# A graph network on one core: waits ahead of GpSimd's gathers are replaced by a small memset ahead of every gather

## The chip, the cores and the metric

One core of a Trainium2 chip runs the whole program. It has five engines with queues of their own: TensorE (matmuls and transposes into PSUM banks), VectorE, ScalarE, GpSimd (which here issues the gathers, as indirect DMAs whose descriptors it writes itself) and SyncE (plain DMAs). Engines wait for one another through semaphores, counters that an instruction increments when it is done. The metric is the device time of one launch in microseconds (us), the median over several runs.

## The reference, cut to what matters

3125 nodes with 128 features; 53125 edges, sorted by their destination node. Two attention layers over the edges, each behind a LayerNorm and a ReLU and with a residual connection:

```
h = relu(layernorm(x));  x = x + layer0(h, src, dst)
    layer0: h = x W^T (8 heads x 16)
            e = leaky_relu(a_src[src] + a_dst[dst]);  alpha = softmax of e over the edges of a node
            out = sum over the edges of a node of alpha * h[src]
h = relu(layernorm(x));  x = x + layer1(h, src, dst, edge_attr)
    layer1: score = q[dst] . k[src] / 4 + edge_attr We;  attn = softmax over the edges of a node
            out = layernorm((sum of attn * v[src]) Wo + residual)
```

For every edge the features of its source node are needed: 544 bytes a row in layer 0 (features and a score part), 1024 bytes in layer 1 (keys and values). That is the gather.

## The kernel before, in words

The edges lie in tiles of 128, one edge a partition. A tile is visited once for each block of 125 destination nodes that it touches; there are 440 visits a layer. 16 visits make a group, 4 visits a quarter: `GROUPS` is 28, the last group has 2 quarters. Each visit has one gather of 128 rows out of a table in HBM into its place in `G` (L532), so there are 440 gathers a layer, 880 in all, 16 in a full group.

`G` holds three groups (`UNROLL = 3`). Group g takes the place of group g - 3, and may fill a quarter of it when VectorE has read that quarter for the last time, in `weigh` (L1418), which increments `pv_ready`. VectorE runs `weigh` of group r = g - 2 in its step g.

All compute engines go through the same steps, one a group, with three groups in work at a time (`run_groups`): in step g the new group g gets its scores, the group g - 1 its maxima and exponentials, the group g - 2 its weighted sums. The order of the work in a step is written out by hand for each engine. What the rows below name:

- TensorE: `spread_ids` (L829, layer 0) or `one_hot_T` (L836, layer 1), counted by `t_done`; `expand` (L851 in layer 0, L849 in layer 1), counted by `expanded`, which brings the values of the destination nodes to the edges; the transposed scores (L883, L884, `scoreT`); the small products `hop1` (L900) and `hop2` (L912); `sums` (L865), 6 batches a group over the 16 visits, counted by `mm_done`.
- VectorE: `add` (L1441), one for each visit, waits for `mm_done` of its batch and adds it to the nodes' sums `acc`; `weigh` (L1418); CCM (L1348) waits for `hop2`; in layer 1 `qk_product` (L1238) waits for a quarter's gathers and for `expand`, `qk_sum` (L1247) sums it, and `sc` (L1291) is the group's score; in layer 0 `score_sum` (L1279) waits for all gathers of the group, and `sc` (L1288) comes behind it.
- ScalarE: copies out of PSUM (ST, L646), one-hot tiles S (L636, L640), exponentials (L673).

GpSimd issues the gathers of a layer in order (`gathers`). Ahead of a quarter it waits for `pv_ready`. Ahead of the first gather of each quarter `pace` has it wait as well for counts of TensorE: `expanded`, `scoreT`, `hop1`, `hop2`, `t_done` of the group before, and `mm_done` of the group that held the place in `G`. These waits aren't needed for the data; the waits on `pv_ready`, on the tables and on the indices are, and stay. Ahead of the gathers of layer 0 GpSimd fills a small tile `pad_i` (1 partition, 2 x 130 columns of int32; L425 to L427), which ScalarE's queue sends to HBM at the start; nobody reads it afterwards.

Of the kernel before, what the change touches and what calls it, by code (L numbers as in the profile page):

```python
# [38 lines left out]
UNROLL = 3  # L39
# [23 lines left out]
NB = len(BATCHES)  # L63
# [12 lines left out]
def gnn_kernel(nc, x, src, dst, edge_attr, w0, att, bias0, wq, bq, wk, bk, wv, bv, we, be, wo, bo, gamma,  # L76
# [3 lines left out]
    def sb(name, shape, dt=F32):  # L80
        return ctx.enter_context(nc.sbuf_tensor(name, shape, dt))

    def sem(name):
        return ctx.enter_context(nc.semaphore(name))

    def wait(eng, s, value):

        if not isinstance(value, int) or value > 0:
            if isinstance(s, Signal):
                eng.wait_ge(s.s, s.base + value)  # L90
            else:
                eng.wait_ge(s, value)

    with ctx:
# [111 lines left out]
        pad_i = sb("pad_i", [1, 2, P + 2], I32)  # L206
# [49 lines left out]
        s_ebout, s_ebin, s_ebt, s_ebe = sem("bias_rows_out"), sem("bias_rows_in"), sem("bias_transposed"), sem("bias_copied")  # L256
        s_ebfin = sem("bias_complete")
        s_out = sem("out_written")
        s_bias3 = sem("bias_parts")
        s_kvb, s_qmm, s_q, s_gain, s_res = (sem(n) for n in (  # L260
            "keys_values_complete", "queries_projected", "queries_complete", "gain_applied", "result"))
# [21 lines left out]
        L = [Layer(0), Layer(1)]  # L283
# [8 lines left out]
        def quarters(g):  # L292

            return 0 if g < 0 or g >= GROUPS else LASTQ if g == GROUPS - 1 else 4
# [119 lines left out]
        def _(pool):  # L414
            n = [0]
# [53 lines left out]
                pool.dma_start(WeBD[ED * c:ED * c + ED, c, :], we).then_inc(s_r, 16)  # L469
            pool.memset(acc[:, :, :], 0.0).then_inc(s_acc0, 1)  # L470

            def pace(n, g, v):

                s, r, q = L[n], g - UNROLL, g - 1
                if v % 4:
                    return
                if g == 0:
                    if v == 12 and n == 0:
                        wait(pool, s["t_done"], 4)
                    return  # L480
                if n == 0:
                    if v == 0:
                        wait(pool, s["expanded"], 4 * q + 2)
                        if r >= 0:
                            wait(pool, s["mm_done"], NB * r + 3)
                    if v == 4:
                        wait(pool, s["expanded"], 4 * q + 4)
                        if r >= 0:
                            wait(pool, s["mm_done"], NB * r + 5)
                    if v == 8:  # L490
                        wait(pool, s["scoreT"], g)
                        if r >= 0:
                            wait(pool, s["mm_done"], NB * r + 6)
                    if v == 12:
                        wait(pool, s["hop1"], g)
                        if r >= 0:
                            wait(pool, s["mm_done"], NB * r + 7)
                elif r < 0:
                    if v == 0:
                        wait(pool, s["expanded"], 4 * q + 1)  # L500
                    if v == 4:
                        wait(pool, s["hop1"], q)
                    if v == 8:
                        wait(pool, s["expanded"], 4 * q + 3)
                else:
                    if v == 4:
                        wait(pool, s["hop1"], q)
                        if r >= 0:
                            wait(pool, s["mm_done"], NB * r + 1)
                    if v == 8:  # L510
                        wait(pool, s["hop2"], q)
                        wait(pool, s["t_done"], 4 * q + 3)
                        if r >= 0:
                            wait(pool, s["mm_done"], NB * r + 3)
                    if v == 12:
                        wait(pool, s["expanded"], 4 * q + 3)
                        wait(pool, s["t_done"], 4 * q + 4)
                        if r >= 0:
                            wait(pool, s["mm_done"], NB * r + 4)

            def gathers(n, table, w):
                s = L[n]

                for g in range(GROUPS):
                    u = g % UNROLL
                    for j in range(quarters(g)):
                        if n == 1 and g == UNROLL - 1 and j == 0:
                            pool.wait_ge(s_ebt, VK * H)
                        wait(pool, s["pv_ready"], 4 * (g - UNROLL) + j + 1)
                        for v in range(QV * j, QV * j + QV):  # L530
                            pace(n, g, v)
                            pool.indirect_dma_start(  # L532
                                G[:, u, v, 0:w], None, table,
                                bass.IndirectOffsetOnAxis(ap=idx_all[:, g * GV + v:g * GV + v + 1], axis=0)
                            ).then_inc(s_gath[u][j], 16)

            pool.wait_ge(s_idx0, 1)
            pool.wait_ge(s_tab[0], 32 * len(CHUNKS))
            gathers(0, table0, W0)
            pool.wait_ge(s_ebout, 16)  # L540
            pool.wait_ge(s_bz, 16)
# [5 lines left out]
            pool.memset(acc[:, :, :], 0.0).then_inc(s_acc0, 1)  # L547
            pool.wait_ge(s_tab[1], 32 * PAIRS)
            gathers(1, table1, W1)


# [1077 lines left out]
```

## Time and profile before

| | |
|---|---|
| median of 3 runs | 1584.45 us (1582.59 to 1594.63) |
| span of the profiled execution | 1585.9 us |
| GpSimd (POOL) busy | 883.4 us, 56% of the span |
| TensorE (PE) busy | 1020.5 us, 64% |
| VectorE (DVE) busy | 934.6 us, 59% |
| ScalarE (ACT) busy | 640.0 us, 40% |
| bytes moved by DMA | 110.35 MB, 70 GB/s |

Of the profiled execution only the span is known; it stands 1.45 us above the median of the runs. "Idle" is the time an engine stood still directly before an instruction, and the name behind the arrow is the releaser, what the profile holds for the end of that wait; "issue" means that nothing it shows ended it, "remote" that the count came from another core or an unknown queue. Matmuls are pipelined, and the ends of their records are modelled.

### The profile page before, as it was taken

The page shows a single profiled execution, that of the slowest core. Times are in us where ns is not written, and L with a number is a line of the kernel's source. Part 1 is how long each engine was busy: PE and PEld are TensorE (multiplying, and loading weights), DVE is VectorE, ACT ScalarE, POOL GpSimd, SP SyncE. Part 2 cuts the span into 40 slices and gives each one's busy share as a digit, 9 for nine tenths or more (in the row PEclk, how much of TensorE's full clock was granted, in tenths as well). Part 3 has the DMA queues.
Part 4 walks back from the last instruction along what each step waited for, and adds up shares of the span by engine and source line. Part 5 has one row for each costly group of instructions (what it writes and reads, how often), then busy time and mean ns, then how long its engine had stood idle before and what let it go on. Part 6 is the DMA issues. An engine that isn't in the chain of part 4 may idle for free.

```text
span 1585.9 us, 21105 instructions
## 1 busy us (share of the span) xinstructions
PE 1020.5 (64%) x4985; PEld 863.7 (54%) x4985; DVE 934.6 (59%) x3002; ACT 640.0 (40%) x1699; POOL 883.4 (56%) x926
## 2 busy tenths in 40 slices
PE   5456666666665766666554577666766676676765
PEld 4345555555554555445354466565655566566664
DVE  6445656556565565557813455656565656656578
ACT  5524334243342433422554234444443434344414
POOL 5766666666666566551046566656666565666500
PEclk9655555555656565566766666877777777777676
DMA  6321222222222222222133222222222222232201
GB/s 138 72 66 43 66 46 66 48 63 45 67 47 67 45 65 47 58 84 57 49 94 95 73 84 84 84 80 80 84 84 84 80 82 81 84 88 83 80 1 41
DMA packets 54202, 110.35 MB, mean 70 GB/s; under 512 B 16876, under 2 KB 30848, under 8 KB 53956
## 3 DMA queue, kind: packets, MB, share of 16 engines
q0 software_dynamic: 36288, 91.12, 22.6%
q1 hardware_dynamic: 16483, 17.39, 4.0%
q8 instruction: 46, 0.75, 0.2%
q14 instruction: 72, 0.59, 0.1%
q10 hardware_dynamic: 1313, 0.50, 0.1%
HBM read 100.60 MB, written 8.81 MB: 69 GB/s over the span
## 4 chain that ended last, share of the span: by engine, by line
DVE 16%; PE 16%; another core or an unknown queue 10%; issue 9%; ACT 2%; DVEq 2%
PE bank L865 6%; PE bank L849 6%; DVE acc L1441 4%; DVE PV L1418 3%; DVE prod L1238 2%; PE bank L836 1%; PE bank L912 1%; DVE raw L1247 1%; DVE halves L1087 1%; PE bank L900 1%; DVEq L1441 1%; ACT S L636 1%; DVEq L1220 0%; DVEq L90 0%
## 5 line engine op out<-in xcount | busy, mean ns | idle before, releaser
L532 POOL DMA_INDIRECT G<-table,idx_all x880 | 857.1, 974 | 544.5 <-issue 280.3
L865 PE MATMUL bank<-PV,S 128*125 128x144 f32 x1760 | 449.5, 416 | 209.5 <-DVE acc L1441 104.4
L865 PEld LDWEIGHTS bank<-PV,S 128*125 128x125 f32 x1760 | 373.9, 287 | 236.1 <-issue 134.9
L1441 DVE TENSOR_TENSOR acc<-acc,bank 125x144 f32 x880 | 260.4, 296 | 339.3 <-remote 191.7
L636 ACT ACTIVATE S<-iota_n,lid 128x125 f32<-128x125 f32 x880 | 275.7, 386 | 0.7 <-issue 0.7
L849 PE MATMUL bank<-qe,ST 125*128 x880 | 182.0, 378 | 87.3 <-DVE prod L1238 80.7
L849 PEld LDWEIGHTS bank<-qe,ST 125*128 125x128 f32 x880 | 164.1, 279 | 96.7 <-issue 95.8
L1418 DVE TENSOR_TENSOR PV<-G,PV 128x512 f32<-128x512 f32 x220 | 151.2, 688 | 23.4 <-issue 22.8
L646 ACT ACTIVATE ST<-bank 125x512 f32<-125x512 f32 x110 | 63.6, 598 | 248.4 <-remote 197.6
L640 ACT ACTIVATE S<-S,ones 128x500 f32<-128x500 f32 x220 | 156.6, 712 | 7.3
L836 PE MATMUL bank<-ident,S 128*125 128x128 f32 x440 | 89.8, 340 | 52.5 <-ACT S L640 31.9
L836 PEld LDWEIGHTS bank<-ident,S 128*125 128x125 f32 x440 | 79.1, 248 | 58.8 <-ACT S L640 35.1
L1228 DVE TENSOR_SCALAR ST<-bank,vcol 125x512 bf16<-125x512 f32 x110 | 81.5, 743 | 32.1 <-remote 27.6
L673 ACT ACTIVATE EP<-DD 128x256 f32<-128x256 f32 (+1 forms) x56 | 20.3, 363 | 191.2 <-DVE DD L1382 191.2
L1238 DVE TENSOR_TENSOR prod<-bank,G 128x512 f32<-128x512 f32 x110 | 74.5, 678 | 30.4 <-PE bank L849 27.1
L1348 DVE TENSOR_TENSOR CCM<-bank,Vsel 128x32 f32<-128x32 f32 x56 | 10.7, 191 | 118.6 <-remote 104.4
L688 ACT ACTIVATE AL<-bank 125x8 f32<-125x8 f32 x56 | 9.9, 177 | 165.9 <-PE bank L957 99.5
L1247 DVE TENSOR_REDUCE raw<-prod 128x32 f32<-128x512 f32 x110 | 74.3, 675 | 1.1
L912 PE MATMUL bank<-D,HselT 8*128 8x16 f32 x224 | 54.4, 358 | 28.8 <-DVE D L1334 27.9
L912 PEld LDWEIGHTS bank<-D,HselT 8*128 8x128 f32 x224 | 48.6, 299 | 42.4 <-DVE D L1334 29.1
L829 PE MATMUL bank<-lid_ring,ones_b 1*125 1x512 bf16 x110 | 53.2, 576 | 9.3 <-ACT attrT L684 5.4
L924 PE MATMUL bank<-WeBD,attrT 128*128 128x32 f32 x208 | 49.1, 400 | 5.6 <-DVE CCM L1348 5.6
(219 smaller groups left out, 1093.8 us busy)
## 6 DMA issues: line engine op xcount, KB each, us to landing
G<-table,idx_all POOLq DMA_INDIRECT x880
prod<-in_edge_attr_dram SPq DMA_DIRECT2D x8, 672.0 KB
table<-G SPq DMA_DIRECT2D x12, 224.0 KB
bias_rows<-qe SPq DMA_DIRECT2D x1, 1664.0 KB
table<-h0b SPq DMA_DIRECT2D x8, 178.5 KB
out_dram<-G SPq DMA_DIRECT2D x8, 168.0 KB
prod<-in_edge_attr_dram SPq DMA_DIRECT2D x8, 90.0 KB
xs<-in_x_dram SPq DMA_DIRECT2D x1, 504.0 KB
```

Of the source, the lines that this page charges most:

```text
L532: pool.indirect_dma_start(G[:, u, v, 0:w], None, table, bass.IndirectOffsetOnAxis(ap=idx_all[:, g * GV + v:g * GV + v + 1], axis=0)).then_ ...
L636: last = act.activation(S[:, u, v, :], iota_n[:, 0:BN], ACT.Abs, bias=lid[:, bass.ds(g * GV + v, 1)], scale=-1.0)
L640: act.activation(S[:, u, QV * j:QV * j + QV, :], S[:, u, QV * j:QV * j + QV, :], ACT.Relu, bias=ones[:, 0:1], scale=-1.0).then_inc(s.sem[" ...
L836: last = pe.transpose(tp[j % 2][0:BN, k * P:k * P + P], S[:, u, QV * j + k, :], ident[:, :])
L849: last = pe.matmul(ex[j % 2][:, k * F:k * F + F], ST[:, v, :], nodes[:, bass.ds(off, F)], start=True, stop=True)
L865: last = pe.matmul(sums_bank(p)[0:BN, at:at + H * SLOT], S[:, ur, v, :], PV[:, v, :, :].rearrange("p h k -> p (h k)"), start=True, stop=True)
L912: last = pe.matmul(sm[:, 64 + GV * k:64 + GV * k + GV], HselT[:, :, :].rearrange("p v h -> p (v h)"), d[:, k, k:k + GV], start=True, stop= ...
L1228: ve.tensor_scalar(ST_b[:, QV * j:QV * j + QV, :], tp[j % 2][0:BN, :].rearrange("p (v e) -> p v e", v=QV), node, None, op0=ALU.is_equal).t ...
L1238: ve.tensor_tensor(prod[:, j % 2, :].rearrange("p (v f) -> p v f", v=QV), ex[j % 2][:, :].rearrange("p (v f) -> p v f", v=QV), G[:, u, QV ...
L1247: ve.tensor_reduce(raw[:, QV * j:QV * j + QV, :].rearrange("p v h -> p (v h)"), prod[:, j % 2, :].rearrange("p (c d) -> p c d", d=DH), AX. ...
L1418: ve.tensor_tensor(PV[:, QV * j:QV * j + QV, :, 0:DH], rows, PV[:, QV * j:QV * j + QV, :, DH:DH + 1].to_broadcast([P, QV, H, DH]), ALU.mul ...
L1441: ve.tensor_tensor(a, a, o, ALU.add).then_inc(s.sem["acc_added"], 1)
```

## The change

`pace` and its calls are taken out. In its place, ahead of every gather, stands `space(260)`: a wait for the memset before it, and a memset of 260 columns of one partition of `pad_i`, which increments a new semaphore. The other waits ahead of gathers stay as they are, and so does every other engine.

```diff
@@ semaphores
+        s_space = sem("spacer_set")
@@ gpsimd
-            def pace(n, g, v):
-
-                s, r, q = L[n], g - UNROLL, g - 1
-                if v % 4:
-                    return
-                if g == 0:
-                    if v == 12 and n == 0:
-                        wait(pool, s["t_done"], 4)
-                    return
-                if n == 0:
-                    if v == 0:
-                        wait(pool, s["expanded"], 4 * q + 2)
-                        if r >= 0:
-                            wait(pool, s["mm_done"], NB * r + 3)
-                    if v == 4:
-                        wait(pool, s["expanded"], 4 * q + 4)
-                        if r >= 0:
-                            wait(pool, s["mm_done"], NB * r + 5)
...
-                else:
-                    if v == 4:
-                        wait(pool, s["hop1"], q)
-                        if r >= 0:
-                            wait(pool, s["mm_done"], NB * r + 1)
-                    if v == 8:
-                        wait(pool, s["hop2"], q)
-                        wait(pool, s["t_done"], 4 * q + 3)
-                        if r >= 0:
-                            wait(pool, s["mm_done"], NB * r + 3)
...
+            spaces = [0]
+
+            def space(width):
+
+                wait(pool, s_space, spaces[0])
+                pool.memset(pad_i[0:1, :, :].rearrange("p a b -> p (a b)")[:, 0:width], 0).then_inc(s_space, 1)
+                spaces[0] += 1
@@ gathers
                         for v in range(QV * j, QV * j + QV):
-                            pace(n, g, v)
+                            space(260)
                             pool.indirect_dma_start(
```

## Rows read from the trace of the kernel before

**Rows 1.** Costliest groups: line engine op, xcount | busy, mean ns | idle before, releaser.
```profile
L532 POOL DMA_INDIRECT G<-table,idx_all x880 | 857.1, 974 | 544.5 <-issue 280.3
...
L1238 DVE TENSOR_TENSOR prod<-bank,G 128x512 f32<-128x512 f32 x110 | 74.5, 678 | 30.4 <-PE bank L849 27.1
```

**Rows 2.** Timeline, a gather behind a gather: start us, us, operation [idle before <-releaser].
```profile
401.25 0.95 POOL L532 DMA_INDIRECT G<-table,idx_all  x1 [0.30 <-issue]
```

**Rows 3.** Timeline, the first and last gather of layer 0, then of layer 1.
```profile
37.62 1.03 POOL L532 DMA_INDIRECT G<-table,idx_all  x1 [9.57 <-DMA table<-h0b]
...
716.11 1.21 POOL L532 DMA_INDIRECT G<-table,idx_all  x1 [0.30 <-issue]
...
799.22 0.96 POOL L532 DMA_INDIRECT G<-table,idx_all  x1 [8.98 <-DMA table<-G]
...
1501.43 1.08 POOL L532 DMA_INDIRECT G<-table,idx_all  x1 [0.30 <-issue]
```

**Rows 4.** Waits: who <- releaser: us in total, times, longest us.
```profile
DVE acc L1441 <- remote: 191.7, 55, 10.2
...
POOL G L532 <- remote: 68.3, 29, 4.1
POOL G L532 <- PE bank L865: 60.2, 32, 5.9
```

**Rows 5.** Timeline of layer 0, around one stall of VectorE and GpSimd.
```profile
424.59 2.74 PE L865 MATMUL bank<-PV,S 128*125 128x144 f32 x10
...
427.20 0.94 POOL L532 DMA_INDIRECT G<-table,idx_all  x1 [0.30 <-issue]
429.82 0.30 DVE L1441 TENSOR_TENSOR acc<-acc,bank 125x144 f32 x1 [5.32 <-remote]
430.47 0.94 POOL L532 DMA_INDIRECT G<-table,idx_all  x1 [2.33 <-remote]
```

**Rows 6.** Timeline, the same wait during the gathers and behind the last one.
```profile
1499.86 0.19 DVE L1348 TENSOR_TENSOR CCM<-bank,Vsel 128x32 f32<-128x32 f32 x1 [3.30 <-PE bank L912]
...
1521.78 0.19 DVE L1348 TENSOR_TENSOR CCM<-bank,Vsel 128x32 f32<-128x32 f32 x1 [1.14 <-PE bank L912]
```

**Rows 7.** Timeline, last gather of a row and first waiter released: row of 4, of 16.
```profile
452.97 0.94 POOL L532 DMA_INDIRECT G<-table,idx_all  x1 [0.30 <-issue]
455.15 0.30 DVE L1441 TENSOR_TENSOR acc<-acc,bank 125x144 f32 x1 [2.84 <-PE bank L865]
...
817.99 0.95 POOL L532 DMA_INDIRECT G<-table,idx_all  x1 [0.30 <-issue]
...
822.02 1.09 ACT L646 ACTIVATE ST<-bank 125x512 f32<-125x512 f32 x2 [3.72 <-remote]
```

**Rows 8.** Timeline of GpSimd, small memsets at the start.
```profile
1.52 0.09 POOL L426 MEMSET pad_i<- 1x2 int32 x1
1.55 0.20 POOL L427 MEMSET pad_i<- 1x130 int32 x1
1.70 0.19 POOL L429 MEMSET ones<- 128x128 f32 x1
```

**Rows 9.** Timeline of VectorE, the last two scores of each layer.
```profile
712.52 0.29 DVE L1288 SCALAR_TENSOR_TENSOR sc<-raw 128x128 f32<-128x128 f32 x1
...
731.56 0.29 DVE L1288 SCALAR_TENSOR_TENSOR sc<-raw 128x128 f32<-128x128 f32 x1
...
1514.52 0.29 DVE L1291 TENSOR_TENSOR sc<-raw,h0b 128x128 f32<-128x128 f32 x1
...
1531.28 0.28 DVE L1291 TENSOR_TENSOR sc<-raw,h0b 128x128 f32<-128x128 f32 x1
```

**Rows 10.** DMA issues: out<-in queue, xcount, KB, median us from issue to landing.
```profile
rowv<-in_L_gnn_bias_dram POOLq DMA_DIRECT2D x1, 62.5 KB, 3.5
```

**Rows 11.** Timeline, first gathers of group 2 and of group 4 of layer 1.
```profile
851.89 0.94 POOL L532 DMA_INDIRECT G<-table,idx_all  x1 [3.97 <-PE bank L849]
...
904.29 0.95 POOL L532 DMA_INDIRECT G<-table,idx_all  x1 [6.25 <-DVE PV L1418]
```

More of the change, by code:

```diff
@@ L470, in _ @@
             pool.memset(acc[:, :, :], 0.0).then_inc(s_acc0, 1)
-            def pace(n, g, v):
-                s, r, q = L[n], g - UNROLL, g - 1
-                if v % 4:
-                    return
-                if g == 0:
-                    if v == 12 and n == 0:
-                        wait(pool, s["t_done"], 4)
-                    return
-                if n == 0:
-                    if v == 0:
-                        wait(pool, s["expanded"], 4 * q + 2)
-                        if r >= 0:
-                            wait(pool, s["mm_done"], NB * r + 3)
-                    if v == 4:
-                        wait(pool, s["expanded"], 4 * q + 4)
-                        if r >= 0:
-                            wait(pool, s["mm_done"], NB * r + 5)
-                    if v == 8:
-                        wait(pool, s["scoreT"], g)
-                        if r >= 0:
-                            wait(pool, s["mm_done"], NB * r + 6)
-                    if v == 12:
-                        wait(pool, s["hop1"], g)
-                        if r >= 0:
[L497 to L500, printed above, removed]
-                    if v == 4:
-                        wait(pool, s["hop1"], q)
-                    if v == 8:
-                        wait(pool, s["expanded"], 4 * q + 3)
-                else:
-                    if v == 4:
-                        wait(pool, s["hop1"], q)
-                        if r >= 0:
-                            wait(pool, s["mm_done"], NB * r + 1)
-                    if v == 8:
-                        wait(pool, s["hop2"], q)
-                        wait(pool, s["t_done"], 4 * q + 3)
-                        if r >= 0:
-                            wait(pool, s["mm_done"], NB * r + 3)
[L515 to L519, printed above, removed]
```

## The prediction

> **What bounds the kernel now.** I read the page's costliest groups, then the waits, then the timeline at single places. GpSimd is busy 857.1 us with 880 gathers and idle 544.5 us ahead of them [rows 1]. No engine is full, so the question is which chain sets the pace of a group of 16 gathers. A gather that follows another one starts 1.25 us after it, 0.95 busy and 0.30 idle [rows 2]. Between the first and the last gather of layer 0 lie 439 steps, from 37.6 to 716.11, which is 678.5 us or 1.546 us a step; in layer 1 they go from 799.22 to 1501.4, 702.2 us or 1.600 [rows 3]. Per full group of 16 that is 24.7 and 25.6 us, of which 20.0 are gathers at 1.25. The rest are pauses: GpSimd stands for counts of TensorE (60.2 us put down to L865), and for a releaser that the profile calls "remote" (68.3) [rows 4]. On one core no other core exists. VectorE too stands 191.7 us, in 55 stalls, for "remote" ahead of its adds at L1441, which wait for TensorE's `mm_done` [rows 4]. So read "remote" as a count that arrived long after the matmul which the profile holds for its source.
>
> The timeline shows it. The ten matmul records that end at 427.33 hold the batch that VectorE's add waits for; the add starts at 429.82 after 5.32 us of idleness, and GpSimd's own gather, which waits for the same batch, at 430.47, after its last one had begun at 427.20 [rows 5]. The same wait, CCM for the four matmuls of L912, stands 3.30 us at 1499.86 while gathers are issued and 1.14 us at 1521.78 when all gathers are over [rows 6]. **Counts of TensorE come late while gathers follow each other closely.** How late depends on how many gathers stood in a row: with four in the row the waiting instruction starts 2.2 us after the last gather's start (452.97, 455.15), with eight 2.6 us (427.20, 429.82), with sixteen 4.0 us (817.99, 822.02) [rows 5, 7]. That is 1.8 us more over 12 gathers, 0.15 us for each. It reads like a queue that needs about 1.25 + 0.15 = 1.40 us for a gather (an estimate from these three places), fills while they come every 1.25 us, and empties in the pauses. Today's pauses, made by the waits on TensorE's counts, empty it twice a group.
>
> **Part 1, the waits are taken out.** Up to four waits a group, 46 groups outside the edges. They cost GpSimd the pauses above. What still stops it is `pv_ready`, the wait for the buffer of three groups ago. Without the waits and with gathers at 1.25 the queue would never be emptied; see the second rival.
>
> **Part 2, 880 memsets of 260 columns of one partition.** Each has a wait for the memset before it, which is long done (a gather lies between), and an increment: nothing on GpSimd beside its own time. Its time: the memset of 2 columns starts at 1.52 and the next starts 0.03 later; that of 130 columns starts at 1.55 and the next instruction at 1.70, 0.15 later [rows 8]. So 0.12 us per 128 columns, and for 260 about 0.03 + 0.24 = 0.27 from start to start. By the durations, 0.09 us for 2 columns and 0.20 for 130, it is 0.31. Bounds for what a step gains: nothing, if the memset fits into the 0.30 us of idleness between two gathers, and 0.31 + 0.35 = 0.66, if the next gather also loses its preparation (third rival). I take 0.285, between 0.25 and 0.31, with the step at 1.25 + 0.285 = **1.535 us**: all gathers and memsets run on the same engine in order, and the 0.30 us stands ahead of nearly every gather without a wait, so I count it as a part of the gather that a memset does not hide. The memset writes one partition of a tile that nobody reads by then; no other engine waits for it. Over 880 that is 251 us more on GpSimd, on an engine that had 544.5 us of idleness.
>
> **Part 3, what comes next.** At 1.535 the gathers come slower than the 1.40 us that the queue needs, so TensorE's counts should be prompt throughout. Then a group needs 16 x 1.535 = 24.6 us on GpSimd, against the chain of the other engines. That chain is seen without late counts at the ends of the layers: from one score instruction to the next 19.0 us in layer 0 (712.52 to 731.56) and 16.8 us in layer 1 (1514.52 to 1531.28) [rows 9]. These steps work on half a group of new edges; a full one adds in layer 1 two products of 0.68 us [rows 1] and two sums of about the same, with TensorE's share of each quarter, say 20 to 21 us in all. The chain stays under 24.6, so GpSimd becomes the bound, continuously issuing. `pv_ready` does not hold it: the buffer that a quarter needs is freed in the step before.
>
> **The sum**, on the profiled span of 1585.9 us. Gathers: 2 x 439 x 1.535 = 1347.7 (now 1380.7), 33.0 less. The ends shrink too, because the work behind the last gather is today further behind than it has to be. After the change the scores of group 26 follow its last gather, which lies 8 steps (12.3 us) before the layer's last one. I give a gather 3.5 us to land (the row of a transfer of the same queue [rows 10]); layer 1 adds 1.7 for a product, a sum and the score, layer 0 some 0.6. Then comes one step as measured: in layer 0, -12.3 + 3.5 + 0.6 + 19.0 = 10.9 us from the last gather to the last score; in layer 1, -12.3 + 3.5 + 1.7 + 16.8 = 9.7. Today these are 731.56 - 716.11 = 15.4 and 1531.28 - 1501.4 = 29.9. So 4.5 and 20.2 less. What lies before the first gather (37.6), between the layers (731.56 to 799.22) and after the last score (54.6) stays. Total: 37.6 + 10.9 + 67.7 + 9.7 + 54.6 = 180.5, and 878 x 1.535 = 1347.7: 1528.2 us. The profiled span stands 1.45 us over the median of the runs (1584.45), so I forecast **1527 us**, 3.6% less. With the step at 1.51 it is 1505, at 1.57 1558; the break-even is at (1585.9 - 180.5) / 878 = 1.601.
>
> **A rule against it.** The rows of L1348 say that TensorE's counts suffer from gathers [rows 6]. "SBUF — State Buffer" of the Trainium skill, section "Who interferes with whom", says the opposite: only the port pair shared by VectorE and GpSimd causes contention, and TensorE and ScalarE never wait on anyone. By that rule spacing the gathers cures nothing, and the lateness would be TensorE's own; that is the first rival.
>
> **Rivals.**
> 1. *The lateness is not the gathers' doing* (matmuls that really end later than the profile models). Then the groups keep their 24.7 and 25.6 us, set by the other engines, and GpSimd at 24.6 fits under them: 1584 us, no change. For it: the ends of matmuls are modelled. Against it: 3.30 against 1.14 us for one and the same wait, and the growth with the length of the row of gathers. Chance 0.08.
> 2. *The memset disappears in the 0.30 us, or the spacing is too small*, and counts are late with no wait left that empties the queue. Then the long unpaced rows set the time. The near rows: groups 2 and 3 of layer 1 held the longest stretch with no wait of this sort, 851.89 to 904.29, 26.2 us a group [rows 11]; at that price for all 46 groups, 23 x 1.5 + 23 x 0.6 = 48 us more: 1632 us. The longest stall of the add, 10.2 us [rows 4] against 5.3 now, once in each of 46 groups, would be its far end, 225 us more. Chance 0.10.
> 3. *Each gather behind a memset starts late*, the mechanism that ends on the other side. At 429.82 and 430.47 two engines react to the same count; the gather needs 0.65 us more than the add, while in a row the gap is 0.30 [rows 5, 2]: so 0.35 us of preparation is hidden under the gather before. If the memset's wait and its place in the queue expose it 880 times, the step is 1.25 + 0.285 + 0.35 = 1.885 and the time 180.5 + 1655 = 1836 us. It decides from a step of 1.60 on. Against it: the memset's count is fulfilled a whole gather earlier. Chance 0.08.
> 4. *The memset is only dearer than its columns*, step 1.60 to 1.70: 180.5 + 878 x 1.65 = 1629 us. Nothing in the trace shows a gather right behind a memset, so this can't be excluded. Chance 0.10.
>
> **How the numbers follow.** The forecast has 0.64, with steps from 1.49 to 1.60 (1488 to 1585 us). About 1% is what a measurement of this kernel tells from no change; that is a step below 1.583 for faster and above 1.619 for slower. Faster: 0.58 of the forecast, 0.03 of rival 1, 0.01 of rival 2: 0.62. Within 1%: 0.06 + 0.04 + 0.02 + 0.02 (rival 4): 0.14. Slower: 0.01 + 0.07 + 0.08 + 0.08: 0.24. The range 1480 to 1615 holds the forecast with a somewhat cheaper memset, rival 1, and the near halves of rivals 2 and 4; outside stay rival 3 and their far halves, about 0.2.
>
> **What the changed profile would show.** Right: memsets of 0.25 to 0.31 us; start to start of gathers near 1.53 with hardly a pause over 2 us from group 6 of each layer on; "remote" all but gone from L1441, L646 and L1348; VectorE waiting instead for a gather's landing, ahead of L1279 and L1238. Wrong: a step over 1.60 (rivals 3, 4); "remote" stalls of 5 us or more (rivals 1, 2); pauses of GpSimd behind L1418, which would mean that the chain of the other engines is longer than 24.6 us.

## The result, and the profile after

The change made the kernel slower: 1645.3 us (median of 4, 1641.0 to 1649.6) against 1588.5 us, ratio 1.033 with the 95% interval 1.029 to 1.038. The forecast was 1527 us. The profiled execution has a span of 1642.9 us, 57.0 more than before.

GpSimd's two groups of instructions on the page after (as [rows 1]; the columns are xcount | busy, mean ns | idle before):

```profile
L492 POOL DMA_INDIRECT G<-table,idx_all x880 | 869.0, 988 | 143.6 <-issue 132.9
...
L478 POOL MEMSET pad_i<- 1x260 int32 x880 | 267.7, 304 | 177.1 <-DVE PV L1378 158.0
```

The memset takes 0.304 us, near the 0.31 us that the durations gave (the sum had 0.285). But the timeline of GpSimd (start us, us) shows what it adds to a step, where [rows 2] had 0.30 us between two gathers:

```profile
424.98 0.95 POOL L492 DMA_INDIRECT G<-table,idx_all  x1 [0.16 <-issue]
425.93 0.30 POOL L478 MEMSET pad_i<- 1x260 int32 x1
426.40 0.95 POOL L492 DMA_INDIRECT G<-table,idx_all  x1 [0.16 <-issue]
427.34 0.30 POOL L478 MEMSET pad_i<- 1x260 int32 x1
427.81 0.95 POOL L492 DMA_INDIRECT G<-table,idx_all  x1 [0.16 <-issue]
```

The memset starts where the gather ends, and the next gather follows 0.16 us after it. Of the 0.30 us, 0.14 vanished under the memset: the step is 1.415 us, not 1.535. The four ends of the layers (as [rows 3]):

```profile
37.76 1.03 POOL L492 DMA_INDIRECT G<-table,idx_all  x1 [0.39 <-issue]
...
724.12 0.95 POOL L492 DMA_INDIRECT G<-table,idx_all  x1 [0.16 <-issue]
...
814.54 0.96 POOL L492 DMA_INDIRECT G<-table,idx_all  x1 [0.16 <-issue]
...
1560.79 0.95 POOL L492 DMA_INDIRECT G<-table,idx_all  x1 [0.16 <-issue]
```

Layer 0 takes 686.4 us from its first to its last gather (678.5 before), layer 1 746.3 (702.2), and everything outside 210.3 (205.2): 7.9 + 44.0 + 5.1 = 57.0. Without a pause 439 steps of 1.415 would be 621 us. So GpSimd still pauses, now at `pv_ready`, where the waits view puts 158.0 us (84.3 before; as [rows 4]):

```profile
DVE acc L1401 <- remote: 173.5, 47, 10.5
ACT ST L606 <- remote: 165.0, 25, 12.5
POOL pad_i L478 <- DVE PV L1378: 158.0, 38, 11.0
```

One such pause in layer 1, from the timeline:

```profile
1471.79 0.97 PE L825 MATMUL bank<-PV,S 128*125 128x144 f32 x6 [1.81 <-DVE acc L1401]
...
1478.16 0.30 DVE L1401 TENSOR_TENSOR acc<-acc,bank 125x144 f32 x1 [5.99 <-remote]
...
1480.97 0.60 ACT L606 ACTIVATE ST<-bank 125x512 f32<-125x512 f32 x1 [11.70 <-remote]
...
1484.28 0.95 POOL L492 DMA_INDIRECT G<-table,idx_all  x1 [0.16 <-issue]
1484.78 0.30 DVE L1401 TENSOR_TENSOR acc<-acc,bank 125x144 f32 x1 [4.39 <-remote]
...
1495.45 0.69 DVE L1378 TENSOR_TENSOR PV<-G,PV 128x512 f32<-128x512 f32 x1 [0.32 <-issue]
1496.20 0.30 POOL L478 MEMSET pad_i<- 1x260 int32 x1 [10.97 <-DVE PV L1378]
```

Read it from below: GpSimd has issued more than a whole group with hardly a pause and then stands 10.97 us for VectorE's `weigh`; VectorE and ScalarE had stood 5.99, 4.39 and 11.70 us for counts of TensorE while the gathers ran. The add at 1484.78 waits for the matmuls of the first line, which ended at 1472.76: 12.0 us pass between the two. The late counts did not go away, and the long pause now comes only when GpSimd has run out of buffers.

The sum of all "remote" stalls is no measure of the loss: over all engines it falls, from 796.8 to 676.2 us. The single count comes later. From the end of a batch's last matmul record to the add that waits for it, the kernel before takes 5.6 us at most, and over 5 us 8 times; the changed kernel takes up to 12.0 us, and over 5 us 25 times.

### The profile page after: what moved, and what is told of

It reads as the page before. It is cut to its first block, busy times and chain, and to the rows that moved or that the text cites. A ratio compares the mean times of both kernels' runs of the same rounds, so it can differ in the third digit from the quotient of the medians.

```text
span 1642.9 us, 21963 instructions
## 1 busy us (share of the span) xinstructions
PE 1010.2 (61%) x4985; PEld 853.2 (52%) x4985; DVE 933.1 (57%) x3002; ACT 636.4 (39%) x1699; POOL 1159.6 (71%) x1806
## 4 chain that ended last, share of the span: by engine, by line
PE 20%; DVE 14%; another core or an unknown queue 10%; issue 8%; ACT 2%; DVEq 1%
PE bank L825 9%; PE bank L809 6%; DVE acc L1401 3%; DVE PV L1378 2%; DVE prod L1198 2%; PE bank L796 2%; PE bank L872 1%; DVE raw L1207 1%; DVE halves L1047 1%; PE bank L860 1%; DVEq L1401 0%; ACT h0b L693 0%; PE bank L949 0%; ACT S L596 0%
## 5 line engine op out<-in xcount | busy, mean ns | idle before, releaser
L492 POOL DMA_INDIRECT G<-table,idx_all x880 | 869.0, 988 | 143.6 <-issue 132.9
L478 POOL MEMSET pad_i<- 1x260 int32 x880 | 267.7, 304 | 177.1 <-DVE PV L1378 158.0
L809 PE MATMUL bank<-qe,ST 125*128 x880 | 175.2, 363 | 143.3 <-DVE prod L1198 120.9
L809 PEld LDWEIGHTS bank<-qe,ST 125*128 125x128 f32 x880 | 154.9, 265 | 154.4 <-issue 153.3
L796 PE MATMUL bank<-ident,S 128*125 128x128 f32 x440 | 95.0, 355 | 60.4 <-ACT S L600 58.5
L796 PEld LDWEIGHTS bank<-ident,S 128*125 128x125 f32 x440 | 84.5, 264 | 66.7 <-ACT S L600 64.2
```

What stands on the lines that cost most here:

```text
L478: pool.memset(pad_i[0:1, :, :].rearrange("p a b -> p (a b)")[:, 0:width], 0).then_inc(s_space, 1)
L492: pool.indirect_dma_start(G[:, u, v, 0:w], None, table, bass.IndirectOffsetOnAxis(ap=idx_all[:, g * GV + v:g * GV + v + 1], axis=0)).then_ ...
L796: last = pe.transpose(tp[j % 2][0:BN, k * P:k * P + P], S[:, u, QV * j + k, :], ident[:, :])
L809: last = pe.matmul(ex[j % 2][:, k * F:k * F + F], ST[:, v, :], nodes[:, bass.ds(off, F)], start=True, stop=True)
```

## Experiments

The runs stood on several chips, and the kernel before was timed on each beside them. Its time differs by chip: 1582.6 us in the first set, 1342.0 in the second, 1559.8 in the third, 1343.6 and 1344.6 in the fourth and fifth. So each kernel is compared inside its own set. No two of the five sets met the same chip, so a lasting property of a chip can't be told here from its state at that hour; "chip" below stands for both.

**First set (before: 1582.6 us).** Each part alone, both together, a wider spacing, and half of the gathers.

e1_none, neither waits nor memset:

```diff
                         for v in range(QV * j, QV * j + QV):
-                            space(260)
                             pool.indirect_dma_start(
```

> Neither the waits on TensorE's counts nor the memset: the removal alone, gathers 1.25 us apart until pv_ready stops them. Theory Q (a queue that needs about 1.4 us for a gather holds TensorE's counts back; spacing at 1.415 us was just too small): the queue fills at 1.25 and nothing empties it but the stops at pv_ready; slower than before, 1640 to 1720 us, near or above the changed kernel, stalls of 8 to 12 us for TensorE's counts. Theory M (the 880 memsets, 268 us of GpSimd, are what costs): 1585 to 1610 us, close to the kernel before.

Measured: 1785.5 us, ratio 1.128 (1.126 to 1.130). Taking the waits out costs 203 us; theory M is dead, and theory Q's 1720 was too low by 65 us. GpSimd's pauses at `pv_ready` and VectorE's stalls for late counts (84.3 and 191.7 us in the trace of the kernel before) both grew:

```profile
POOL G L491 <- DVE PV L1377: 495.7, 99, 28.1
DVE acc L1400 <- remote: 438.2, 49, 10.3
```

e2_both, the waits stay and the memset is added:

```diff
                             pace(n, g, v)
+                            space(260)
                             pool.indirect_dma_start(
```

> The waits on TensorE's counts stay and the memset of 260 columns is added. Theory Q: gathers at 1.415 us with two pauses a group, so the queue is nearly always empty; counts prompt, a group takes 16 x 1.415 = 22.6 us plus short waits, 1500 to 1570 us, faster than before. Theory M: today's pauses stay and 268 us of memsets come on top of a GpSimd that is paced already, 1600 to 1660 us.

Measured: 1570.9 us, ratio 0.992 (0.991 to 0.994), just over what theory Q expected and far under theory M's 1600. 268 us more of work on GpSimd cost nothing; the kernel is 0.8% faster. But the counts were not prompt, against theory Q: VectorE's add still stood 164.1 us for "remote". A step of 1.415 us doesn't make the counts prompt even with the pauses.

e3_two128, the changed kernel with a second memset:

```diff
                 pool.memset(pad_i[0:1, :, :].rearrange("p a b -> p (a b)")[:, 0:width], 0).then_inc(s_space, 1)
-                spaces[0] += 1
+                pool.memset(w0n[0:1, 0:128], 0.0).then_inc(s_space, 1)
+                spaces[0] += 2
```

> The changed kernel with a second memset of 128 columns behind the first, so a gather every 1.55 to 1.57 us and no wait on TensorE's counts. Theory Q: above 1.4 to 1.5 us the queue never fills; counts prompt, GpSimd issues without a pause, time 180.5 + 878 x 1.56 = 1550 us (1540 to 1565). Theory M: 125 us more of memsets on GpSimd, 1690 us or more, with TensorE's counts as late as in the changed kernel.

Measured: 1579.9 us, ratio 0.998 (0.997 to 0.999). This is one of two runs that the cause rests on (the other is e12_two4b, below). On the chip on which e1_none took 1785.5 us, 441 us of memsets made the kernel 206 us faster: the waits view has not one line with "remote", every add that waits for a batch starts no more than 0.14 us behind the end of the batch's last matmul record (up to 11.8 us in e1_none), and VectorE waits for gathers to land instead:

```profile
ACT ST L607 <- PE bank L797: 280.5, 53, 10.0
...
DVE raw L1240 <- DMA G<-table,idx_all: 232.7, 27, 13.4
...
DVE prod L1199 <- DMA G<-table,idx_all: 144.1, 42, 4.9
```

GpSimd is the bound, as forecast for the change itself, but the time is 30 us over the expected 1550. The step between two plain gathers is 1.56 us; the mean over a layer is more (start us of its first and last gathers, and one long gather in layer 0):

```profile
37.62 1.03 POOL L493 DMA_INDIRECT G<-table,idx_all  x1 [0.28 <-issue]
...
307.66 1.63 POOL L493 DMA_INDIRECT G<-table,idx_all  x1 [0.16 <-issue]
...
741.82 0.95 POOL L493 DMA_INDIRECT G<-table,idx_all  x1 [0.16 <-issue]
...
818.48 0.97 POOL L493 DMA_INDIRECT G<-table,idx_all  x1 [0.16 <-issue]
...
1514.46 0.95 POOL L493 DMA_INDIRECT G<-table,idx_all  x1 [0.16 <-issue]
```

That is 1.604 and 1.585 us a step. In layer 0 about one gather in a group takes 1.6 in place of 0.95 us; in layer 1 such gathers are fewer, 9 over 1.3 us, and the rest of the excess lies in smaller delays. Outside the gathers lie 1577.5 - 704.2 - 696.0 = 177.3 us, against 180.5 in the sum.

e4_half, half of the gathers from the fourth group on:

```diff
                         for v in range(QV * j, QV * j + QV):
-                            space(260)
+                            if v % 2 and g >= UNROLL:
+                                continue
                             pool.indirect_dma_start(
...
-            return 16 * QV * (i + 1 + n * rounds)
+            return 8 * QV * (i + 2 + n * (rounds + 1))
```

> No waits, no memset, and from the fourth group of each layer on only every second gather is issued (the others' rows are stale, so the sums are not the reference's). It shows the chain of the other engines without late counts. Theory Q: 8 gathers a group come in short rows; counts prompt, a group takes 18 to 19 us in layer 0 and 20 to 21 in layer 1, about 1290 to 1330 us in all. If the late counts are TensorE's own, the groups keep 25 us and the time stays at 1560 to 1600 us.

Measured: 1344.9 us in a single run, 15 us over theory Q's range. VectorE's add stood 0.5 us for "remote" in all. Other waits still show it, 208 us in all: most of it lies at the layers' starts, where all gathers are issued, but now and then a CCM still stands up to 3.6 us, to the end of the run. The chain of the other engines with hardly a late count, from score to score in layer 0 and in layer 1:

```profile
270.11 0.29 DVE L1249 SCALAR_TENSOR_TENSOR sc<-raw 128x128 f32<-128x128 f32 x1
...
288.09 0.29 DVE L1249 SCALAR_TENSOR_TENSOR sc<-raw 128x128 f32<-128x128 f32 x1
...
967.87 0.29 DVE L1252 TENSOR_TENSOR sc<-raw,h0b 128x128 f32<-128x128 f32 x1
...
989.33 0.29 DVE L1252 TENSOR_TENSOR sc<-raw,h0b 128x128 f32<-128x128 f32 x1
```

18.0 and 21.5 us a group, against 24.7 and 25.6 in the kernel before, for the same work of TensorE: the lateness came with the gathers.

**Second set (before: 1342.0 us).** A finer sweep of the spacing: e3's edit with `w0n[0:1, 0:4]`, `0:40` and `0:80`, and gathers of 64 rows. It met a chip on which nothing is ever late.

> The changed kernel with a second memset of 4 columns: a gather every 1.44 to 1.45 us in place of 1.415. Theory Q puts the limit between 1.415 (counts late) and 1.560 (none late). If it lies under 1.445: counts prompt, 177.3 us outside the gathers + 878 x (1.445 + 0.035) = 1477 us (the 0.035 is what the steps of the run at 1.560 took more on average). If above: still late counts, 1600 to 1640 us. A rival, theory A (lateness falls smoothly with the spacing), expects 1615 to 1630.

> The same with a second memset of 40 columns: 1.475 us. Theory Q with the limit under it: 177.3 + 878 x 1.51 = 1503 us and no late count. Theory A (smooth): some 1610 us with a part of the counts late.

> The same with a second memset of 80 columns: 1.51 us. Theory Q: 177.3 + 878 x 1.545 = 1534 us and no late count, about 2.9% under the run at 1.560. Theory A: 1595 us.

Measured: 1491.4, 1502.9 and 1552.8 us, ratios 1.111, 1.120 and 1.157 (each within 0.002). No "remote" line in any of them, and the time rises with the step, GpSimd being the bound; the sums were short by 14 and 19 us for the first and the last and right for the second. But the kernel before took 1342 us there, so these runs say nothing of the limit.

e8_rows64 leaves the space out and gathers 64 rows:

```diff
-                            space(260)
+                            m = P if g < UNROLL else 64
                             pool.indirect_dma_start(
-                                G[:, u, v, 0:w], None, table,
-                                bass.IndirectOffsetOnAxis(ap=idx_all[:, g * GV + v:g * GV + v + 1], axis=0)
+                                G[0:m, u, v, 0:w], None, table,
+                                bass.IndirectOffsetOnAxis(ap=idx_all[0:m, g * GV + v:g * GV + v + 1], axis=0)
```

> No waits, no memset, and from the fourth group of each layer on every gather brings only the first 64 rows (the other partitions keep stale rows, so the sums are not the reference's). It asks what fills the queue. If it is the number of rows (descriptors), a gather needs some 0.7 us of it and the gathers come every 0.8 to 1.0 us: counts are prompt, about 1330 to 1350 us as with half the gathers. If it is something that each gather does once, whatever its rows, the gathers come faster than 1.4 us apart and counts are as late as with neither waits nor memset, 1650 us or more.

Measured: 1330.3 us in a single run on the chip without late counts, so inconclusive.

**Third set (before: 1559.8 us).** The kernel before for its trace, the changed kernel, e1's and e5's again.

> The kernel before, once more, for its trace beside the others of this call. The second set of runs stood on another chip, where the kernel before took 1342 us and no count of TensorE was late in any run. Theory C (whether gathers hold TensorE's counts back differs from chip to chip): on a chip of that kind 1340 to 1345 us, stalls for 'remote' under 20 us in all; on a chip of the first kind 1580 to 1590 us with the stalls of the profile shown. A rival, theory D (that chip is faster in everything): the stalls remain and each instruction is shorter.

> The changed kernel, once more. Theory C on a chip without late counts: GpSimd alone bounds it, 177.3 + 878 x (1.415 + 0.035) = 1450 us, 8% slower than before there. On a chip with late counts 1640 to 1650 us, 3.5 to 4% slower.

> Neither waits nor memset, once more. Theory C on a chip without late counts: the chain of the other engines bounds it, 17.9 us a group in layer 0 and 21.5 in layer 1 as in the run with half the gathers, or GpSimd with 16 x 1.25 = 20 where that is longer: 1320 to 1345 us, no slower than before. On a chip with late counts 1785 us, 12.8% slower.

> The changed kernel with a second memset of 4 columns, a gather every 1.45 us, once more. On a chip with late counts this is what the second set was to tell: with a limit under 1.45 us some 1490 us, 6% faster than before; with a limit above it late counts and 1560 to 1640 us. On a chip without them 1491 us, 11% slower than before.

Measured: before 1560.3 us; changed 1556.5, ratio 0.997 (0.993 to 1.001), no difference; neither part 1847.2, 1.184 (1.177 to 1.190); step of 1.45 us 1495.0, 0.958 (0.954 to 0.962), the fastest complete kernel on any chip with late counts. I had given the changed kernel 1640 to 1650 us and the kernel with neither part 1785 us on such a chip: both missed, the size of the lateness differs from chip to chip. The stalls of the add at a step of 1.415 (first line) and of 1.45 us (second):

```profile
DVE acc L1401 <- remote: 195.3, 74, 8.8
```

```profile
DVE acc L1402 <- remote: 21.3, 14, 2.9
```

This is the changed kernel itself beside one whose gathers start 0.04 us further apart, on one chip: over all engines the "remote" stalls fall from 540.8 to 88.7 us, and the time by 61 us, though GpSimd has more to do. A single wider memset was not run, so the second memset and the wider step are not told apart.

The whole step of e12_two4b: the second memset costs 0.09 us by its duration and moves the next gather by 0.04.

```profile
502.77 0.95 POOL L493 DMA_INDIRECT G<-table,idx_all  x1 [0.16 <-issue]
503.71 0.30 POOL L478 MEMSET pad_i<- 1x260 int32 x1
503.97 0.09 POOL L479 MEMSET w0n<- 1x4 f32 x1
504.22 0.95 POOL L493 DMA_INDIRECT G<-table,idx_all  x1 [0.16 <-issue]
```

**Fourth and fifth set (before: 1343.6 and 1344.6 us).** Both met chips without late counts.

> Gathers of 64 rows from the fourth group of each layer on, no waits, no memset, once more, since its first run stood on a chip where no kernel had late counts. On a chip with late counts: if rows (descriptors) fill the queue, a gather of 64 needs 0.7 us of it and comes every 0.9 to 1.2 us: counts prompt, 1320 to 1350 us. If each gather costs the same whatever its rows, counts are late as with neither waits nor memset: 1700 us or more. On a chip without late counts 1330 us again, which tells nothing.

> A second memset of 40 columns, a gather every 1.475 us, once more. On a chip with late counts, where 1.45 us left 40% of layer 0's counts late by over 1 us though GpSimd hardly paused: theory Q has the limit between 1.45 and 1.56, so few or none late here; GpSimd bounds the time either way, 1500 to 1515 us. If the limit lies above 1.475, counts stay late and the time is 1500 to 1560.

> The kernel before again for its trace. On a chip without late counts: stalls for 'remote' under 20 us in all, a group in 18 to 21.5 us, 1342 us. On one with late counts 1555 to 1595 us.

> The changed kernel, for the kind of chip that it has not met yet. Without late counts GpSimd bounds it: 177.3 + 878 x (1.415 + 0.035) = 1450 us, 8% slower than the 1342 to 1346 us of before there. On a chip with late counts between the two results so far, 1556 and 1645 us.

> Neither waits nor memset. On a chip without late counts the chain of the other engines or GpSimd at 1.25 us sets the time: 1320 to 1345 us, so neither the waits nor the memset would be of use there. On a chip with late counts 1785 to 1850 us.

> Gathers of 64 rows, for a chip with late counts. If the rows fill the queue: counts prompt, 1320 to 1350 us. If each gather costs the same whatever its rows: late counts, 1700 us or more. On a chip without late counts 1328 us.

Measured: gathers of 64 rows 1327.1 and 1319.5 us, telling nothing of the queue; the step of 1.475 us 1503.9 us, ratio 1.121 (1.116 to 1.125); before 1346.4; the changed kernel 1463.6, 1.087 (1.085 to 1.089), 13 us over the sum for a GpSimd that bounds alone, with the step of 1.415 and e3's 0.035 on it; neither part 1343.4, 0.999 (0.997 to 1.001). The kernel before on such a chip has no "remote" line. Its costliest wait of GpSimd and its add, beside [rows 4]:

```profile
POOL G L532 <- issue: 241.6, 793, 0.3
...
DVE acc L1441 <- PE bank L865: 124.0, 106, 1.6
```

Theory D is dead: the stalls do not remain. Its gathers take 990 ns in the mean, those of [rows 1] 974, and `weigh` 685 ns against 688. TensorE's records are shorter (L849 336 ns against 378, at a granted clock of 0.693 against 0.666), but that comes with prompt counts and not with the chip: in the first set, on one chip, the same matmul takes 407 ns in e1_none and 312 in e3_two128. What is missing there is the lateness, and with it 240 us.

## Why the prediction was wrong

- *What bounds the kernel* was read rightly. "Remote" is TensorE's counts arriving late, and gathers close to each other are what makes them late: e3, e4 and e12 show it; in e3 no count of a batch comes over 0.14 us behind the matmul records.
- *Part 1* was costed at nothing but its pauses, on the condition that the spacing holds. Alone it costs 203 us in the first set and 287 in the third, and 0 where no count is late. Where counts are late, the pauses were worth more than they cost.
- *Two steps failed together, Part 2's step and the limit of Part 3.* In Part 2 I took the 0.30 us between two gathers for a part of the gather that a memset doesn't hide. 0.14 of it was hidden: 0.95 + 0.304 + 0.16 = 1.415, where the sum had 1.535. I held the bound "nothing" for possible and weighed it too low; the truth lay between. This alone doesn't give the result: with 1.415 us against the limit of 1.40 the prediction's own sum is 180.5 + 878 x 1.415 = 1422.9 us, 220 us under what was measured.
- *The limit* was put at 1.40 us and is higher. The estimate came from three places that compare waits of two engines for different matmuls, and had no margin beside 1.415. At 1.415 the counts are late on the chip of the result, on that of the first set (e2) and on that of the third, at 1.45 much less is left on the latter (stalls of the add 195.3 to 21.3 us), at 1.56 nothing on that of the first set. One fixed limit is not shown, nor is the queue itself, and its place may differ by chip: at 1.45, 46 of the 114 counts that an add waits for still come over 0.5 us behind the matmul records, up to 4.0 us.
- *Part 3 and the sum* hold where their condition holds. e3 gives a GpSimd that is the bound and 177.3 us outside the gathers for 180.5; the chain is 18.0 and 21.5 us for "19" and "20 to 21". The sum lacked the long gathers and the smaller delays, 0.025 to 0.045 us a step or 31 us in all. `pv_ready` doesn't hold GpSimd there, as forecast; with late counts it does.
- *The rivals.* The second came true with its mechanism, late counts in long rows that end only at `pv_ready`, and I had given it 0.10. That its price of 1632 us comes near 1645 is partly luck: it was taken from rows with gathers 1.25 us apart, 26.2 us a group, where this step is 1.415 and the layers take 25.0 and 27.2; really unspaced rows took 26.7 and 30.5 (e1_none). The first is dead by e3. "SBUF — State Buffer" of the Trainium skill, section "Who interferes with whom", has TensorE wait for nobody. The waits view has no line of TensorE for "remote" in any run, which agrees; but its counts arrive late, 12.0 us in the changed kernel, on the chips of the result, of the first and of the third set, and that depends on the spacing of the gathers.

That the same change is 3.3% slower, no different and 8.7% slower on three chips is explained by two prices: 1.415 us a step on GpSimd, which is always paid (8.7% where it is all), and the late counts that the memset prevents compared with those that the waits prevented. The first is measured; the second is read from the difference. What makes a chip one or the other, and whether the rows of a gather or the gather itself fill the queue, stays open. So does what the gathers hold up: no run tells the descriptors that GpSimd writes from the traffic of the rows. No version that was run beats both kernels everywhere: a step of 1.45 us does on the one chip with late counts where it ran (0.958), and is 11% slower without them; the kernel before loses nothing against e1_none there, so its waits cost nothing where they are not needed.

## What to carry to other kernels

Idleness between two instructions of an engine is not a price that an instruction put between them adds to; look at how a short one sits there, or bound the step from the duration alone (here 1.25 to 1.56 us) and ask what happens at each end of it. When a change replaces a wait that paces an engine by a fixed spacing, the spacing has to be right on every chip, while the wait adapts; and where the forecast rests on a threshold, the estimate of the threshold needs an interval too.

## What was not expected of the hardware

- The same kernel takes 1342 us on some chips and 1560 to 1588 us on others, with the same durations of VectorE's instructions and of the gathers to 2%. The difference goes with counts of TensorE that arrive late while GpSimd issues gathers.
- 880 memsets that compute nothing made the kernel without waits 140 us faster (1785.5 us in the first set, 1645.3 for the changed kernel on the chip where it was first timed, with 1582.6 and 1588.5 for before), and 291 us faster in the third set (1847.2 to 1556.5).
- A memset of 4 columns behind one of 260 takes 0.09 us and moves the next gather by 0.04.
